# A two-layer image and text transformer on one core: routing of layer 0 with early text norms, Newton roots and gates on GpSimd

## The reference

```python
h = tok(x)                                   # patches: layernorm, W, layernorm, + position
h = jnp.concatenate([h, txt], axis=1)        # 16 x 165 x 256
h = h + attn0(layernorm(h))                  # selective scan, times gelu(z), then W_out + b_out
# ffn of layer 0 on xf = layernorm(h):
macro = sigmoid(xf @ macro_w)                # 4 groups; the largest is taken
mv = top1(macro); mv = mv / (mv + 1e-9)
micro = sigmoid(einsum('td,gde->tge', xf, micro_w))   # 2 experts per group, both taken
uv = micro / (sum(micro) + 1e-9)
w = mv * one_hot(group) * uv
out = einsum('te,tef,efd->td', w, silu(xf @ gate_w) * (xf @ up_w), down_w)
h = h + out
h = h + attn1(layernorm(h))                  # causal softmax attention with rotary embedding
h = h + moe1(layernorm(h))                   # 4 experts, top 2, gelu
```

## Time and profile before

| | |
|---|---|
| median of 3 runs | 805.38 us (804.9 to 805.58) |
| profiled execution, first to last instruction | 803.3 us |
| TensorE busy | 707.5 us (88%) |
| VectorE busy | 472.0 us (59%) |
| ScalarE busy | 374.7 us (47%) |
| GpSimd busy | 355.7 us (44%) |
| mean granted TensorE clock | 0.945 |
| DMA | 66.02 MB, mean 82 GB/s |

### The profile page before, as it was taken

The page is one execution under the profiler, slowest core; times in us unless marked ns, Lnnn a source line. Parts: engine busy times, 40 slices in busy tenths (PEclk is TensorE's granted clock), DMA queues, the critical chain, the costliest instruction groups (busy, mean ns, idle before and its releaser), DMA issues.

```text
span 803.3 us, 16716 instructions
## 1 busy us (share of the span) xinstructions
PE 707.5 (88%) x5182; PEld 568.7 (71%) x5183; DVE 472.0 (59%) x1213; ACT 374.7 (47%) x881; POOL 355.7 (44%) x310
## 2 busy tenths in 40 slices
PE   3988960899999999997988999589999999999991
PEld 2757950466666666665877988478888888888871
DVE  4898798643433333335789897946544545554540
ACT  5797557333333333333455764724344344344430
POOL 3429980123222322220666874034555556555331
PEclk9997995899999999997999999789999999999996
DMA  9970044041211121115312234512232333232335
GB/s 267 413 290 1 1 142 148 27 114 27 37 27 26 28 38 26 26 20 158 100 53 79 81 99 141 182 41 41 47 46 47 53 53 49 44 47 45 40 35 149
DMA packets 37177, 66.02 MB, mean 82 GB/s; under 512 B 3776, under 2 KB 29360, under 8 KB 35568
## 3 DMA queue, kind: packets, MB, share of 16 engines
q1 hardware_dynamic: 23696, 46.90, 17.6%
q0 software_dynamic: 13248, 18.21, 14.4%
q10 hardware_dynamic: 192, 0.38, 0.1%
HBM read 44.83 MB, written 23.35 MB: 85 GB/s over the span
## 4 chain that ended last, share of the span: by engine, by line
PE 70%; DVE 16%; ACT 5%; DMA 3%; issue 2%; POOL 2%; POOLq 0%; SPq 0%; DVEq 0%
PE PS L788 15%; PE PS L981 15%; PE PS L994 15%; PE PS L806 8%; PE PS L1349 3%; PE PS L796 3%; DVE tops L734 2%; PE PS L1376 1%; ACT Y L2000 1%; PE PS L966 1%; DMA Y<-in_wtok_dram 1%; DVE h L2504 1%; PE PS L2151 1%; POOL X L1598 1%; PE PS L1357 1%
## 5 line engine op out<-in xcount | busy, mean ns | idle before, releaser
L788 PE MATMUL PS<-X,Y 128*128 x576 | 133.7, 382 | 1.1 <-DVE Y L886 1.1
L1160 POOL DMA_INDIRECT sum<-X,dest x45 | 88.5, 1967 | 96.9 <-ACT X L1063 81.4
L994 PE MATMUL PS<-X 128*128 x720 | 125.7, 273 | 1.9 <-ACT X L1063 1.9
L981 PE MATMUL PS<-X 128*128 128x256 f16 (+1 forms) x768 | 122.6, 265 | 0.7 <-issue 0.7
L1053 ACT ACTIVATE X<-PS,X 128x256 f32<-128x256 f32 (+1 forms) x192 | 72.8, 463 | 103.3 <-PE PS L981 100.2
L952 POOL DMA_INDIRECT sum<-Y,dest x24 | 38.1, 1586 | 148.3 <-ACT Y L863 148.3
L897 DVE SCALAR_TENSOR_TENSOR Y<-PS,Y 128x512 f32<-128x512 f32 x48 | 36.1, 751 | 111.4 <-PE PS L788 111.2
L981 PE MATMUL PS<-X,Y 128*128 128x256 f16 (+1 forms) x384 | 100.1, 264 | 0.0
L788 PEld LDWEIGHTS PS<-X,Y 128*128 128x128 f16 x576 | 56.8, 99 | 60.3 <-issue 3.5
L994 PE MATMUL PS<-Y,X 128*128 x360 | 98.2, 273 | 0.0
L981 PEld LDWEIGHTS PS<-X 128*128 x768 | 71.8, 97 | 10.7 <-issue 1.3
(11 more groups left out here) (398 smaller groups left out, 1410.2 us busy)
## 6 DMA issues: line engine op xcount, KB each, us to landing
X<-in_w_dram SPq DMA_DIRECT2D x11, 1024.0 KB, 16.6
stage<-in_w_dram SPq DMA_DIRECT2D x16, 512.0 KB, 3.6
sum<-h SPq DMA_DIRECT2D x2, 2048.0 KB, 7.6
xs<-Y SPq DMA_DIRECT2D x2, 1040.0 KB, 5.6
xs<-Y SPq DMA_DIRECT2D x2, 1032.0 KB, 6.0
h<-in_txt_dram SPq DMA_DIRECT2D x2, 1024.0 KB, 17.2
Y<-in_patches_dram SPq DMA_DIRECT2D x3, 672.0 KB, 8.2
sum<-h SPq DMA_DIRECT2D x2, 768.0 KB, 6.3
```

Source lines behind the costliest of these rows:

```text
L788: ins = nc.tensor.matmul(PS[:, 2 * u + s, 0:F0], x_[:, slot, k, :], w_[:, at_:at_ + F0], start=(n == 0), stop=(n == 3 * KC - 1))
L981: ins = nc.tensor.matmul(PS[:, 2 * s + c // 2, (c % 2) * T1:(c % 2) * T1 + tokens], part[:, off:off + P], x_[:, slot, k, 0:tokens], start= ...
L994: ins = nc.tensor.matmul(PS[:, 4 + a, 0:D], h_[:, s, c, a * P:(a + 1) * P], part[:, off:off + D], start=(s == 0 and c == 0 and n == 0), st ...
L1160: nc.gpsimd.indirect_dma_start(out=sum1, out_offset=bass.IndirectOffsetOnAxis(ap=dest[:, i:i + 1], axis=0), in_=y1buf[:, u % 2, i - first_ ...
```

## The change

- **Start.** TensorE's wait for `wt_loaded` moves from ahead of the first transposes to ahead of the first product.
- **Image bias.** The one addition over six image tiles becomes one tile in each of iterations 1 to 6.
- **Text scales.** In iteration 8, `newton(0, BATCH)` computes root and shift of the 16 text tiles on VectorE. ScalarE norms text rows between and behind its last high halves: chunk 21, two rows, 22, two rows, 23, two rows, then ten more.
- **Sigmoid table.** A Sigmoid of one column, whose result nothing reads, follows those rows and loads the table. The Sigmoid of the logits comes next and the six image rows behind it.
- **Image scales.** `newton(BATCH, IT)` takes the place of `scales` behind the loop; ScalarE's square root there goes.
- **Gates.** VectorE's gate operations go, but for one reciprocal, which moves into `positions` ahead of the slot maps (`meanwhile`) and waits for GpSimd. VectorE's wait for the Sigmoid stays where it was. GpSimd computes the rest in `pool_gates0` between its last split and its first gather, and signals `pay_ready`. SyncE's program is the same.
- Two semaphores are added. `nega_ready` goes, and the weights' twelve load semaphores become seven: loads from the third on share one by two, so their users wait for both. Counts of `scales_ready` in layer 1 go up by one.

The diff, without the declarations and counts of semaphores:

```diff
@@ -154,6 +154,16 @@
     return isinstance(i, int) and i == value
+
+
+def w0_group(m):
+
+    return m if m < 2 else 1 + m // 2
+
+
+def w0_landed(m):
+
+    return 16 if m < 2 else 32
@@ -685,6 +696,8 @@
             chain.link(nc.vector.tensor_scalar(first_of, pos[:, 0:choices, :], -P, None, ALU.bitwise_and))
+            if meanwhile:
+                meanwhile()
             n = choices * NT
@@ -1195,17 +1208,12 @@
-        def act_rest(act, roots, normal):
-            roots()
-            act.wait_ge(scales_ready, 6)
-
-            def norm_row(t):
-                normal(pay[:, t, 0:D], h[:, t, :], t, P).then_inc(pay_normed, 1)
-            for t in range(2):
-                norm_row(t)
+        def act_rest(act, roots, normal, norm_row):
+            nc.scalar.activation(amax[:, 1:2], k_row, ACT.Sigmoid)
             act.wait_ge(logits_ready, 1)
             nc.scalar.activation(rb[:, :, :], ra[:, :, :], ACT.Sigmoid).then_inc(sig_ready, 1)
-            for t in range(2, NT):
+            act.wait_ge(scales_ready, 7)
+            for t in range(BATCH, NT):
                 norm_row(t)
@@ -1223,7 +1231,31 @@
+        def pool_gates0(pool, chain):
+
+            pool.wait_ge(choice_ready, 1)
+            pool.wait_ge(sig_ready, 1)
+            score, a, u, chosen = ra[:, 4, :], ra[:, 5, :], ra[:, 6:8, :], ra[:, 8:12, :]
+            micro = rb[:, 4:12, :].rearrange("p (g e) t -> p e g t", e=E0)
+            for of, to in ((micro[:, 0], u[:, 0, :]), (micro[:, 1], u[:, 1, :]), (rb[:, 0:4, :], score)):
+                chain.link(nc.gpsimd.tensor_tensor(chosen, of, oh[:, 0], ALU.mult))
+                chain.link(nc.gpsimd.tensor_tensor(chosen[:, 0:2, :], chosen[:, 0:2, :], chosen[:, 2:4, :], ALU.add))
+                chain.link(nc.gpsimd.tensor_tensor(to, chosen[:, 0, :], chosen[:, 1, :], ALU.add))
+            nc.gpsimd.tensor_scalar(chosen[:, 0, :], score, 1e-9, None, ALU.add)
+            chain.link(nc.gpsimd.tensor_tensor(a, u[:, 0, :], u[:, 1, :], ALU.add))
+            chain.link(nc.gpsimd.tensor_scalar(a, a, 1e-9, None, ALU.add))
+            nc.gpsimd.tensor_tensor(a, a, chosen[:, 0, :], ALU.mult).then_inc(gate_sums, 1)
+            for e in range(E0):
+                ins = nc.gpsimd.tensor_tensor(u[:, e, :], u[:, e, :], score, ALU.mult)
+            chain.link(ins)
+            pool.wait_ge(gate_sums, 2)
+            for e in range(E0):
+                ins = nc.gpsimd.tensor_tensor(pay[:, :, D + e], u[:, e, :], a, ALU.mult)
+            ins.then_inc(pay_ready, 1)
+
         def pool_rest(pool):
+            chain = Chain(pool, pool_done)
+            pool_gates0(pool, chain)
             pool_slots0(pool)
@@ -1239,32 +1271,18 @@
                 chain.link(nc.vector.tensor_tensor(raw, raw, tmp, ALU.subtract))
-            scales(0, NT, off_mean)
+            newton(BATCH, IT, off_mean)
             nc.vector.tensor_tensor(ra[:, :, :], raw, over_tiles(rstd[:, :]), ALU.mult).then_inc(logits_ready, 1)
-            top, score, a, b = rc[:, 8, :], rc[:, 9, :], rc[:, 10, :], rc[:, 11, :]
+            top = rc[:, 8, :]
             chain.link(nc.vector.tensor_scalar(rc[:, 0:4, :], ra[:, 0:4, :], SAT, None, ALU.min))
             first_max(chain, rc[:, 0:4, :], top, oh[:, 0], oh[:, 1], rc[:, 4:8, :])
+            def divide():
+                dve.wait_ge(gate_sums, 1)
+                nc.vector.reciprocal(ra[:, 5, :], ra[:, 5, :]).then_inc(gate_sums, 1)
             dve.wait_ge(sig_ready, 1)
-
-            chain.link(nc.vector.tensor_reduce(score, rb[:, 0:4, :].rearrange("p g t -> p t g"), AX, ALU.max))
-            chain.link(nc.vector.tensor_scalar(a, score, 1e-9, None, ALU.add))
-            chain.link(nc.vector.reciprocal(a, a))
-            chain.link(nc.vector.tensor_tensor(score, score, a, ALU.mult))
-            u = ra[:, 0:2, :]
-            micro = rb[:, 4:12, :].rearrange("p (g e) t -> p e g t", e=E0)
-            for e in range(E0):
-                chain.link(nc.vector.tensor_tensor(rc[:, 0:4, :], micro[:, e], oh[:, 0], ALU.mult))
-                sum_over(chain, u[:, e, :], rc[:, 0:4, :])
-            chain.link(nc.vector.tensor_tensor(a, u[:, 0, :], u[:, 1, :], ALU.add))
-            chain.link(nc.vector.tensor_scalar(a, a, 1e-9, None, ALU.add))
-            chain.link(nc.vector.reciprocal(a, a))
-            chain.link(nc.vector.tensor_tensor(a, a, score, ALU.mult))
-            for e in range(E0):
-                chain.link(nc.vector.tensor_tensor(pay[:, :, D + e], u[:, e, :], a, ALU.mult))
-            dve.sem_inc(pay_ready, 1)
-            positions(dve, chain, 1, SLOT0, 0, inrow0, intile0, 1)
+            positions(dve, chain, 1, SLOT0, 0, inrow0, intile0, 1, divide)
             for e in range(len(TOPS_AT), G0 * E0 - 2):
@@ -1965,7 +1983,7 @@
                 else:
-                    pool.wait_ge(w0_loaded[n // 2], 16)
+                    pool.wait_ge(w0_loaded[w0_group(n // 2)], w0_landed(n // 2))
                     if n >= 2:
@@ -2123,9 +2141,18 @@
                 ins.then_inc(g_ready, 1)
-            for n in range(chunk, XW // CW):
+            def norm_row(t):
+                normal(pay[:, t, 0:D], h[:, t, :], t, P).then_inc(pay_normed, 1)
+
+            rest = range(chunk, XW // CW)
+            for n in rest:
                 high_half(n)
-            act_rest(act, roots, normal)
+                act.wait_ge(scales_ready, 6)
+                norm_row(2 * (n - chunk))
+                norm_row(2 * (n - chunk) + 1)
+            for t in range(2 * len(rest), BATCH):
+                norm_row(t)
+            act_rest(act, roots, normal, norm_row)
@@ -2145,6 +2172,8 @@
                 pe.wait_ge(patch_copied, j + 1)
+                if j == 0:
+                    pe.wait_ge(wt_loaded, 16)
                 if j >= 3:
@@ -2153,7 +2182,6 @@
             pe.wait_ge(consts_loaded, 16)
-            pe.wait_ge(wt_loaded, 16)
             for j in range(IT):
@@ -2514,10 +2542,12 @@
                     chain.link(ins)
-                if i == 1:
-                    add_bout(BATCH, IT)
+                if 1 <= i <= IT:
+                    add_bout(BATCH + i - 1, 1)
                 if i == BATCH // 2 - 1:
-                    dve.wait_ge(bout_added, 3)
+                    dve.wait_ge(bout_added, 2 + IT)
+                if i == BATCH // 2:
+                    newton(0, BATCH)
                 if i in TOPS_AT:
```

More of the change, by code:

```diff
@@ L380, in build @@
         xnt_ready = sem("xnt_ready")
+        pool_done = sem("pool_done")
+        gate_sums = sem("gate_sums")
         text_tr = sem("text_tr")
@@ L389, in build @@
         w0_split = sem("w0_split")
-        w0_loaded = [sem(f"w0_loaded{i}") for i in range(XW // CW // 2)]
+        w0_loaded = [sem(f"w0_loaded{i}") for i in range(w0_group(XW // CW // 2 - 1) + 1)]
         consts_ready = sem("consts_ready")
@@ L396, in build @@
         std_ready = sem("std_ready")
-        nega_ready = sem("nega_ready")
         patch_normed = sem("patch_normed")
@@ L630, in dest_of_token, with positions @@
             chain.link(nc.vector.tensor_tensor(to, to, from_, ALU.add))
-        def positions(dve, chain, choices, tiles, done, inrow, intile, unit):
+        def positions(dve, chain, choices, tiles, done, inrow, intile, unit, meanwhile=None):
             hot = rc[:, 0:4, :]
@@ L1549, in norm @@
             def norm(b, asked):
-                act.wait_ge(scales_ready, 6 + asked)
+                act.wait_ge(scales_ready, 7 + asked)
                 act.wait_ge(xn_tr, NF + b + 1)
@@ L1796, in act_layer1 @@
         def act_layer1(act, roots, normal):
-            act.wait_ge(scales_ready, 11)
+            act.wait_ge(scales_ready, 12)
             def norm_row(t):
@@ L1921, in _ @@
                 to = X[:, at + 2 * CW:at + 4 * CW] if m < XW // CW // 2 - 1 else stage.rearrange("p a n -> p (a n)")
-                sp.dma_start(to, w0[:, at:at + 2 * CW]).then_inc(w0_loaded[m], 16)
+                sp.dma_start(to, w0[:, at:at + 2 * CW]).then_inc(w0_loaded[w0_group(m)], 16)
             sp_rest(sp)
@@ L2003, in _ @@
             chain.link(nc.scalar.activation(c_nega, c_alog, ACT.Exp))
-            nc.scalar.mul(c_nega, c_nega, -1.0).then_inc(nega_ready, 1)
+            nc.scalar.mul(c_nega, c_nega, -1.0)
             def norm_patch(j):
@@ L2107, in high_half @@
             def high_half(n):
-                act.wait_ge(w0_loaded[n // 2], 16)
+                act.wait_ge(w0_loaded[w0_group(n // 2)], w0_landed(n // 2))
                 act.wait_ge(w0_split, n - 1)
```

## The result

The changed kernel takes 812.12 us (median of 5 runs, 810.66 to 814.32) beside 805.38 on the same chip (804.55 to 807.67): ratio 1.0098, 95% interval 1.0079 to 1.0118. The prediction was 813.0. The profiled run was the longest of the five, 814.32 with a span of 812.5, so its excess of 9.2 over the span of before is larger than the 6.7 of the medians.

What follows compares the result with a forecast made beforehand. Before the first expert, VectorE's loop, ScalarE's norms and the last row store were taken to bound; TensorE behind. Landing +8.1 with start -0.5 gave +7.6: 805.4 + 7.6 = 813.0, eight in ten 807.5 to 817.

Steps and rivals of the forecast that it cites:

- Start: Ahead of the loop: moving the token-weights wait behind the first transposes gains 0.5 us, bounds -2.0 and +0.2.
- Loop: VectorE's output loop: six bias additions, their waits for GpSimd and text Newton end it 6.1 us later, bounds +0.8 and +11.3.
- The +0.8 without any wait: VectorE's output loop: with five additions and text Newton but no wait, it ends at 119.3 instead of 118.49.
- Newton for text: Iteration 8 on VectorE: eleven operations take 2.3 us, no wait added as GpSimd has run dry, up to 2.1 otherwise.
- the Sigmoid tie: Ahead of `positions`: ScalarE's 12.0 us up to the Sigmoid tie with VectorE's 11.9, nothing added, bounds 0 and +1.
- Roots +0.85, gates -5.24: Behind the loop: image roots on VectorE add 0.85 us, gates leaving VectorE save 5.24; one-hot copy done at 130.3.
- Gates on GpSimd: Behind the one-hot copy: gate columns ready 6.7 us later, at 137.0, including 1.3 for SBUF sharing; before, ready at 128.0.
- Stores: SyncE's three row stores, held for the gate columns, go at once and land 10.9 us later, bounds 10.6 and 11.8.
- Rival A: Loop and gates: little contention, loop +0.8 to +3, columns 5.4 to 6 after the copy; +1.5 to +4.5, 808.4; 25%.
- Rival B: VectorE's additions: the wait passes over several GpSimd operations, three more of 2.1 us; +14, 819; chance 10%.
- Rival C: Start: VectorE's 1.59 us wait vanishes and its chain passes GpSimd's cast, -2.0 to -4; 803 to 805; chance 7%.
- D: Rival at the stores: gates don't hold them, columns come as early as before; no change but for the loop; 3%.

Runs made afterwards that it cites:

- the second profile: Profile of the changed kernel run once more, unedited, beside its relatives on one chip: 814.04 us, ratio 1.0107 to the kernel before.

## Why the prediction came out right

1. *Start, -0.5.* The second pass came 0.52 earlier, but that is chance: the edit alone did nothing. The term should have been 0.
2. *Loop, +6.1.* Measured +6.4 and, in the second profile, +7.1. The additions make 4.3 of it in both profiles without Newton, Newton the rest. In the first profile the parts fit: the waits of iterations 2 to 6 were 0.8, 1.9, 0.1, 1.9 and 0.15 (additions less 0.28), in sum 4.9 for my 5.3, and the walk of 2.0, 2.0, 0.1, 2.0, 0.1 missed only the first. In the second they don't: the waits of these additions were 3.2 in sum, the additions took 0.91 on average, under the 1 us that I had named as the sign, and 3.7 of wait stood in Newton, where I had none. That the sum held there is luck as far as my working goes. The +0.8 without any wait was too low as well: the loop that has none is 2.2 longer than before (36.25), because VectorE, once it is no longer late, waits for TensorE (1.17 and 0.64). I had read that VectorE never waits for TensorE again after the long addition, but not that it is the faster of the two and was working off its delay, which is why most of the 3 us of wait in the kernel before cost nothing. And my rule that any VectorE operation on SBUF waits is too wide: scans and moments don't.
3. *Newton for text, 2.3 and no wait; the Sigmoid tie.* Right in the first profile (115.67 to 117.94), wrong in the second, where GpSimd had not run dry yet and two operations waited 1.87 each. ScalarE needed 11.7 from the scales (117.94 to 129.67), and VectorE was held 0.23 by the Sigmoid. That no wait came is a matter of phase: in the other kernels with VectorE earlier an operation took 2.0 and 4.4.
4. and 5. *Roots +0.85, gates -5.24.* The copy ended at 130.26, forecast 130.3.
6. *Gates on GpSimd, 6.7 behind the copy.* 6.65 in the changed kernel and in five built on it. The split inside it was off: sharing stretched the thirteen operations by little (0.22 to 0.40 each), but the two products into the strided columns took 1.26 where I had 0.5 with the hand-over.
7. *Stores, 10.9.* 10.6 to the landing, 10.87 to the gather. With the stores apart 0.5 to 0.6 of the 1.0% came back, the larger half. The same stores took 11.0 to 12.0 to the landing in four other profiles, two of them above my bound of 11.8.

Together +7.7 at the landing against +8.1. Rival A fell: its loop of +0.8 to +3 came in neither profile, though in the second the additions alone were nearer to it than to the forecast. Rival B was half there: the first addition waited over four pieces of GpSimd's until their run ended at 88.54, and Newton's first in another kernel over two more operations, but the loop's total stayed at the forecast. Rival C fell with the start alone, D with the stores at 136.94. What I did not price is the clock behind a longer idle stretch, a part of the 1.5 in the profile.

## What to carry to other kernels

Price a transfer by what releases it: a few columns that come late hold all the megabytes that are stored with them, and storing them apart gave back as much here as moving their arithmetic back (0.5% each). Before work is split into pieces or given to another engine, see which of the two shares its path to SBUF with a neighbour; six short operations met four waits of 0.8 to 2.6 us in one profile where one met one. A saving on an engine that waits for another, or is nearly level with it, is to be priced by the other one's pace. And a stage's length that comes out as forecast does not show that its parts did: here the waits moved from the additions to Newton from one profile to the next.

## What the runs showed of the hardware

- A VectorE operation waits for GpSimd's two-input operation when it reads two SBUF inputs (0.42 with one in PSUM, 2.2 without), and also when it has a single float32 input, if the output is in SBUF too (1.97, 2.04 and 4.37 for 16 columns; 0.18 with the output in PSUM, in both kernels that have it so). Scans of 2048 float16 columns and moments beside the same operations never stretched (2.28, 0.74). The Trainium skill (SBUF — State Buffer, section "SBUF: two separate sides") names two kinds that contend with GpSimd, an operation in a two-port mode and one with two SBUF inputs; the trace agrees on the second, and for the first no row names an operation's mode. By it the loser waits until the instruction that holds the pair ends, and the 4.37, in which two further GpSimd operations went ahead, disagrees.
- A store of 2,816 pieces of 8 bytes, 22 KB, took 4.97 to 5.88 us from issue to landing, of which the DMA share accounts for some 1.3 us of traffic. The three stores of 2.9 MB took 10.9 to 12.3 from the gate columns to the gather.
- TensorE came back to 2.4 GHz ahead of the second pass at 77 in one profile of the changed kernel and at 83 in the other. VectorE's second pass moved with it (3.3 and 6.1 us behind the first), and with that its arrivals among GpSimd's operations.
- Profiles of kernels with nearly the same code ahead of it started the output loop's second pass at any time from 78.5 to 85.1, so that a single profile's span says little on a change of 0.3%.
